# Side stages of the ten half-size-product steps put into other slots of a hand-ordered transformer kernel

## The reference, cut to what matters

```python
x = x + _L0_xattn_ref(_layernorm(x), ctx_4096, ctx_4096, mask_BxSxS2_ff1, wq, wk, wv, wo)
x = x + _L0_ffn_ref(_layernorm(x), qweight_gu, ..., scales_down, g_idx_down)
x = x + _L1_xattn_ref(_layernorm(x), ctx_4096, mask_1x1xSxS2_ff0, ...)
x = x + _L1_ffn_ref(_layernorm(x), Wq, Wr, aux_keys, aux_values, ...)

# _L0_ffn_ref: 4-bit weights, 512 -> 2 x 1376 -> 512
w_gu = scales[g] * (nibble(qweight_gu) - zeros[g])        # 512 x 2752
gate, up = split(x @ w_gu)
h = silu(gate) * up
w_d = scales[g] * (nibble(qweight_down) - zeros[g])       # 1376 x 512
out = h @ w_d
```

## Time and profile before

| what | us |
|---|---|
| median of 3 runs (2410.39 to 2413.1) | 2411.44 |
| the profiled execution, time | 2413.45 |
| the profiled execution, span of the instructions | 2411.7 |
| mean granted TensorE clock | 0.993 of full speed |
| busy: VectorE, ScalarE, GpSimd | 1695.2, 1287.7, 1315.3 |

### The profile page before, as it was taken

The page is one execution under the profiler, slowest core; times in us unless marked ns, Lnnn a source line. Parts: engine busy times, 40 slices in busy tenths (PEclk is TensorE's granted clock), DMA queues, the critical chain, the costliest instruction groups (busy, mean ns, idle before and its releaser), DMA issues.

```text
span 2411.7 us, 46184 instructions
## 1 busy us (share of the span) xinstructions
PE 2356.1 (98%) x18020; PEld 1333.2 (55%) x18028; DVE 1695.2 (70%) x3229; ACT 1287.7 (53%) x2511; POOL 1315.3 (55%) x1069
## 2 busy tenths in 40 slices
PE   8899999999999999999989999999999999999998
PEld 4555555555555555444666655555555555555554
DVE  8877776777777788656777576666666666765666
ACT  7666555556555555434444554555555555544453
POOL 4556666666666666237843354445555555445631
PEclk9999999999999999999999999999999999999999
DMA  6111121312121111011102111122121212221101
GB/s 212 45 45 36 45 54 27 123 27 54 31 55 30 44 40 29 27 44 36 42 14 78 48 32 27 45 54 62 36 62 36 62 36 62 53 43 27 27 14 70
DMA packets 217911, 116.59 MB, mean 48 GB/s; under 512 B 169408, under 2 KB 192608, under 8 KB 216672
## 3 DMA queue, kind: packets, MB, share of 16 engines
q1 hardware_dynamic: 217696, 113.64, 18.5%
HBM read 65.81 MB, written 8.39 MB: 31 GB/s over the span
## 4 chain that ended last, share of the span: by engine, by line
PE 60%; POOL 15%; DVE 13%; ACT 6%; issue 5%; DMA 0%; SPq 0%; POOLq 0%; DVEq 0%; ACTq 0%
PE PB L945 17%; PE PB L897 16%; PE PB L881 6%; POOL AR L2933 5%; PE PB L1057 4%; PE PB L1114 4%; POOL AR L2938 4%; PE PB L1068 3%; POOL PSP L2951 3%; DVE WB L2115 2%; PE PB L922 2%; PE PB L987 2%; DVE AR L2313 2%; ACT JUNK L1455 1%; PE PB L853 1%
## 5 line engine op out<-in xcount | busy, mean ns | idle before, releaser
L945 PE MATMUL PB<-WB,AR 128*128 128x512 f16 x3072 | 683.3, 380 | 1.5 <-DVE AR L2313 1.1
L897 PE MATMUL PB<-XTB,WB 128*128 128x512 f16 x3072 | 681.0, 380 | 2.3 <-DVE WB L2115 1.3
L945 PEld LDWEIGHTS PB<-WB,AR 128*128 128x128 f16 x3072 | 297.8, 98 | 355.2 <-issue 5.9
L897 PEld LDWEIGHTS PB<-XTB,WB 128*128 128x128 f16 x3072 | 298.0, 98 | 347.7 <-issue 8.5
L2944 POOL TENSOR_TENSOR AR<-AR,SML 128x512 f32<-128x512 f32 x128 | 144.6, 1151 | 317.9 <-DVE SML L2298 317.9
L2328 DVE SCALAR_TENSOR_TENSOR X<-PB,SML,X 128x512 f32<-128x512 f32 x256 | 189.5, 747 | 170.1 <-PE PB L945 164.0
L1617 ACT ACTIVATE AR<-PB 128x512 f16<-128x512 f32 x256 | 131.3, 596 | 223.8 <-PE PB L987 223.8
L2208 DVE TENSOR_TENSOR AR<-PB,AR 128x512 f16<-128x512 f32 x128 | 88.2, 690 | 164.3 <-ACT AR L1580 164.3
L2933 POOL TENSOR_TENSOR AR<-AR,CST 128x512 f32<-128x512 f32 x128 | 183.0, 1429 | 31.3 <-ACT AR L1527 31.3
L1533 ACT ACTIVATE AR<-AR 128x512 f16<-128x512 f32 x128 | 80.5, 630 | 197.1 <-POOL AR L2938 195.7
L2179 DVE TENSOR_TENSOR AR<-AR 128x512 f16<-128x512 f32 x128 | 132.4, 1035 | 71.8 <-ACT AR L1533 71.8
(11 more groups left out here) (312 smaller groups left out, 4081.1 us busy)
## 6 DMA issues: line engine op xcount, KB each, us to landing
STG<-in_wo SPq DMA_DIRECT2D x14, 1024.0 KB
STG<-in_wq SPq DMA_DIRECT2D x13, 1024.0 KB
STG<-in_qw_gu SPq DMA_DIRECT2D x40, 128.0 KB
STG<-in_ctxT SPq DMA_DIRECT2D x4, 1024.0 KB
X<-in_x SPq DMA_DIRECT2D x4, 1024.0 KB, 10.4
kept<-CTB SPq DMA_DIRECT2D x4, 1024.0 KB, 8.2
CTB<-kept SPq DMA_DIRECT2D x4, 1024.0 KB, 6.2
out_x<-X SPq DMA_DIRECT2D x16, 256.0 KB, 2.4
```

Of the source, the lines that this page charges most:

```text
L897: m = pe.do.matmul(b[:, :], wq[x][:, k, h * 128:(h + 1) * 128], XT[y][c][:, k, :], start=n == 0, stop=n == 11)
L945: m = pe.do.matmul(b[:, :], AT[x][:, h, t * 128:(t + 1) * 128], wo[y][:, h, :], start=n == 0, stop=n == 11)
```

## The change

Six tables of slots are changed, and nothing else. By engine queue:

- `unpack_d` of the second half of blocks 3 and 4 goes from slot (s,3,2) to (s,3,3), s = 2 and 3.
- Token sums of chunk 0: `fold_x` goes from (2,0,2) and (2,0,3) to (2,0,3) and (2,1,1), `fold_x_hi` from (2,1,1) to (2,1,3), `fold_x_lo` from (2,1,2) and (2,1,3) to (2,2,0) and (2,2,1).
- Token sums of chunk 1: `join_x` goes from (2,3,0) and (2,3,1) to (2,2,3) and (2,3,0), `fold_x` from (2,3,2) and (2,3,3) to (2,3,1) and (2,3,2), `fold_x_hi` from (3,0,1) to (2,3,3), `fold_x_lo` from (3,0,2) and (3,0,3) all to (3,0,0).
- The weights w(1,0,1) and w(1,0,2) (s = 2 and 3): `scale` goes from (s,3,2) to (s+1,0,0), `low` from (s,3,3) and (s+1,0,0) to (s+1,0,1) and (s+1,0,3).
- The weight w(1,1,1): `amax` goes from (4,3,1) to (4,3,0).

```diff
-                plan_f(*(((0, 3, 3), (1, 0, 1))[j] if s == 0 else (1, 2 + j, 3) if s == 1 else (s, 3, 2 * j)), "unpack_d", s + 1, j)
+                plan_f(*(((0, 3, 3), (1, 0, 1))[j] if s == 0 else (1, 2 + j, 3) if s == 1 else (s, 3, 3 * j)), "unpack_d", s + 1, j)
...
-            (0, ((2, 0, 0), (2, 0, 1), (2, 0, 2), (2, 0, 3), (2, 1, 1)), ((2, 1, 2), (2, 1, 2), (2, 1, 3), (2, 1, 3))),
-            (1, ((2, 3, 0), (2, 3, 1), (2, 3, 2), (2, 3, 3), (3, 0, 1)), ((3, 0, 2), (3, 0, 2), (3, 0, 3), (3, 0, 3))),
+            (0, ((2, 0, 0), (2, 0, 1), (2, 0, 3), (2, 1, 1), (2, 1, 3)), ((2, 2, 0), (2, 2, 0), (2, 2, 1), (2, 2, 1))),
+            (1, ((2, 2, 3), (2, 3, 0), (2, 3, 1), (2, 3, 2), (2, 3, 3)), ((3, 0, 0), (3, 0, 0), (3, 0, 0), (3, 0, 0))),
...
-        for s in (1, 2, 3):
-            plan_prep_f(w(1, 0, s - 1), (s, 2, 3), (s, 3, 1), (s, 3, 2), (s, 3, 3), (s + 1, 0, 0))
+        plan_prep_f(w(1, 0, 0), (1, 2, 3), (1, 3, 1), (1, 3, 2), (1, 3, 3), (2, 0, 0))
+        for s in (2, 3):
+            plan_prep_f(w(1, 0, s - 1), (s, 2, 3), (s, 3, 1), (s + 1, 0, 0), (s + 1, 0, 1), (s + 1, 0, 3))
...
-        plan_prep_f(w(1, 1, 1), (4, 3, 1), (4, 3, 2), (4, 3, 3), (5, 0, 1), (5, 0, 2))
+        plan_prep_f(w(1, 1, 1), (4, 3, 0), (4, 3, 2), (4, 3, 3), (5, 0, 1), (5, 0, 2))
```

## The result

The changed kernel takes 2416.43 us (median of 17 runs, 2413.07 to 2418.51), the kernel before 2412.27 us on the same chip (17 runs, 2408.39 to 2416.33). The ratio is 1.0014, 95% interval 1.0007 to 1.0020: slower by 3.4 us, 1.7 to 4.8 (the two medians themselves lie 4.2 us apart). The forecast was 6.0 us faster. The profiled execution has a time of 2415.40 us, a span of 2413.6 and a mean granted clock of 0.994.

A forecast was written before the change was run, and what follows sets the result against it. TensorE, busy 98% of the span, bounds the kernel. -5.3 us at the end of (3,1), -0.9 at (4,0) and +0.2 for thin margins give -6.0: 2411.44 to 2405.4 us; 8-in-10 range 2401.0 to 2411.0.

The forecast's parts named there:

- The step that failed: (4,3): Step (4,3): the 1.1 us wait for the squares' load stays; DVE's queue shifts 3.4 us, costing nothing, at worst 1 us.
- The rival that ended slower: ScalarE's queue, scale delaying the copy of P5 in (3,0) and (4,0): +2.4 us, 2413.8; chance 0.12, 0.08 past the bound.
- the tables in (3,0), 0.7 us: In (3,0) the tables wait for banks 4 and 5 from 1195.4 until 1196.1, after DVE's unpack_d.
- 0.6 for a hidden quarter: Duration used for a hidden quarter on DVE: 0.6 us, with 0.69 as the mean, less where GpSimd is idle.
- The rival with stalls that cost the clock: Stalls of (3,0) longer or followed by half clock, 1.7 us a stretch: gain 2.5 to 4 us, 2408.2; chance 0.18.
- My reason against it: Against half clock in (3,0): in both stalls TensorE works at full rate before and after.
- The other stalls of (3,0): In (3,0) P7 waits 1.5 us for the P6 sum, and 2.5 us are lost waiting for the first down tile.
- 1190.0, as forecast: In (2,3) DVE adds P7 only after POOL's add_p5 ends at 1188.0; the three sums end at 1190.0.
- (4,0): The 0.9 us wait goes; scale delays the copy of P5 by 4.9 us, nothing lost, margin 0.6, up to 0.6 lost.
- waiting for TensorE again in (3,2): Later wants of (3,1) have 0.6 to 1.6 us to spare, and in (3,2) DVE waits for TensorE again.
- the removal: In (3,1) P6 follows P1 at once, at 1211.1 and full clock; the 36 matmuls are done 5.3 us ahead.
- Chunk 0: The 0.6 us wait in (2,1) goes; 4.8 us more on DVE in (2,2) are hidden, with margins of about 1 us.

The follow-up runs named there:

- experiment 3: The changed kernel with the small matmul of the first preparation (l1) in PSUM bank 5 instead of 4; ratio to the kernel before 0.9990.
- experiment 1: The changed kernel with the sum of squares of w(1,1,1) back in slot (4,3,1); ratio to the kernel before 0.9994.
- kernel 2: The kernel before with one edit alone, the sum of squares of w(1,1,1) moved to slot (4,3,0); ratio to the kernel before 1.0014.
- kernel 6: Experiment 1's kernel with scale and low parts of w(1,0,1) and w(1,0,2) back in their old slots; ratio to the kernel before 0.9991.
- experiment 4: Experiment 1's kernel with unpack_d of block 3's second half behind the sums' high parts in ScalarE's queue; ratio to the kernel before 0.9989.
- experiment 7: Experiment 1's kernel with unpack_d of the second half of blocks 3 and 4 back in slot (s,3,2); ratio to the kernel before 0.9982.
- Experiment 5: The kernel before with only the token sums of chunk 1 in their new slots; ratio to the kernel before 0.9990.
- experiment 9: The kernel before with only the token sums of chunk 0 in their new slots; ratio to the kernel before 1.0009.

## Why the prediction was wrong

**The step that failed: (4,3).** It said that moving `amax` ahead "does not move the landing, so the 1.1 us stay", that DVE's queue shifts by 3.4 us, and the P3 sum is just in time: "Nothing, at worst 1 us". That the shift reaches the P3 sum with next to nothing was right, by experiment 3. What was left out is a reader inside the shifted queue: DVE's reduction of the first small matmul, and the bank that the two small matmuls share. I followed the shift to the one place where a product's bank comes free and took it for the only one. It cost 4.8 us by the ledger, 1.3 of them the load's later landing in this execution, and 4.4 and 4.5 us by experiments 1 and 2. The rival that ended slower had the right mechanism, ScalarE's queue in front of the copy of P5, in the wrong step, (3,0), and by `scale` and not by a load.

**Mis-sized: the tables in (3,0), 0.7 us.** It came to 1.89 us of wait and 1.5 us of half clock (4.26 for 2.76). The cause of the longer wait is the term "0.6 for a hidden quarter"; this is read off the rows, no run was made for it. DVE's timeline of the changed kernel in (2,3), with the joins and differences running on GpSimd beside it (second fence):

```profile
1188.85 1.40 DVE L2445 SCALAR_TENSOR_TENSOR AR<-AR,SML 128x256 f32<-128x256 f32 x1
...
1190.77 0.89 DVE L2445 SCALAR_TENSOR_TENSOR AR<-AR,SML,WB 128x256 f32<-128x256 f32 x1
1191.58 1.49 DVE L2445 SCALAR_TENSOR_TENSOR AR<-AR,SML,PSP 128x256 f32<-128x256 f32 x1
```
```profile
1185.50 1.26 POOL L3037 TENSOR_TENSOR WB<-WB,PSP 128x512 f32<-128x512 f32 x1
...
1187.35 5.43 POOL L3016 TENSOR_TENSOR WB<-WB 128x512 f32<-128x512 f32 x4
```

The three take 3.78 us, 2.0 more than 3 x 0.6; the mean of the earlier trace rows hid that such an operation takes 0.5 us beside an idle GpSimd (at 1210.16 and 1212.05 of this trace) and 0.9 to 1.5 beside a busy one here, and the change moved GpSimd's work right beside them. I had used this contention for the low parts and not for the quarters. `unpack_d` then ended 1.6 us later than forecast, and the wait grew by 1.2, as P1 of (3,0) itself was 0.5 us late.

The Trainium skill (SBUF — State Buffer, "Who interferes with whom") says that a DVE operation with two SBUF inputs is held up by a GpSimd operation that reads SBUF. By that rule the quarters should stretch too, and these rows agree; I named the rule only for the low parts.

**Mis-sized: the clock.** The rival with stalls that cost the clock had 0.18 and a price of 1.7 us; it happened, behind the 1.89 us wait, at 1.5 us. In the stalls that follow at 0.53 and 1.69 us the clock stayed at 1.00. My reason against it, full rate before and after, did not hold. That the clock falls behind a wait of this size is not certain either: in (4,3) of kernel 6 TensorE waited 1.88 us, also from full rate, and the 36 matmuls behind it ran at 1.00 and took 3.93 us.

```profile
1308.31 0.22 PE L1004 MATMUL PB<-IDB,SML 128*128 128x128 bf16 x1 [1.88 <-ACT JUNK L1456]
```

The Trainium skill (TensorE: Matmul & The Clock Gate, "HAM oscillation — how this bites in real kernels") warns of longer idle gaps only, and by it the forecast would have stood; the 0.50 behind a wait of 1.89 us differs from it, and the measurement decides.

**The other stalls of (3,0)** came where forecast and shorter: 0.53 us for 1.5, and 1.69 for 2.5, as the tables had already eaten their part. By experiments 4 and 6 the down tile's is ScalarE's queue, as the prediction had it. `add_p5` ends at 1186.76 (1185.50 + 1.26), and VectorE's P7 sum starts 0.09 us behind it, at 1186.85 (the profile names no releaser there); the P3 sum is done at 1188.87. With the 1.14 us by which this execution came in earlier that is 1190.0, as forecast.

**(4,0).** The 0.9 us went, and 1.1 us came (1269.61), where the margin was given as 0.6 us. It takes two edits together, since neither experiment 6 nor 7 has it: `unpack_d`'s high part, now in slot (3,3,3), lets ScalarE copy P1 only at 1260.31, 2.7 us after P1's end, and `scale` follows with its 4.9 us as forecast. The prediction doesn't say when it had that copy start, so what it charged for the high part can't be read off it; the quarter behind them took 1.19 us, not 0.6, which alone uses up the margin. A loss of 0.7 us in (3,3) was not in the prediction: the small matmul's bank 4 is held by `unpack_d` for 0.31 us, and the down product starts 0.8 us after P2's end, where it was 0.1 (1246.78 now, 1250.20 before). Experiments 1, 3, 4 and 7 have this wait and 6 has not, so it comes with the move of `scale` and its low parts. The prediction had VectorE waiting for TensorE again in (3,2); in the trace it waits there only for ScalarE (1.18 us) and GpSimd (1.13 us), and is still behind in (3,3).

**Right:** the removal. The 5.3 us wait and the half clock in (3,1) went; P6 followed P1 at once, at 1212.00, which is 1213.1 on the clock of the kernel before (+ 1.14), 2.0 us behind the 1211.1 forecast. Experiment 5 shows it to be the work of the one row of chunk 1. **Chunk 0** was expected to be free and to bring 0.6 us; in experiment 9 it brings these and costs 1.6, of which 0.9 by the start of (3,0) and 0.6 in it. Its price on VectorE was forecast right: in the changed kernel VectorE leaves (2,2) at 1177.42, 1178.6 on the clock of before, as the prediction has it. What it left out is again the reader of a small matmul's bank, in (2,3).

**Open:** how much of the 3.4 us by the runs, against 2.8 by the trace, lies outside these steps, since each kernel was profiled in one execution; and why the clock fell behind 1.89 us of idle time in (3,0) and not behind 1.88 us in (4,3) of kernel 6.

## What to carry to other kernels

An in-order queue that meets a load has everything behind it at the landing's mercy. When an instruction that waits for a DMA is moved ahead, list every reader behind it on that engine and on the engines that follow it, the small ones too, and for each ask which buffer or PSUM bank it frees and who takes that next. And cost an operation by its duration beside the neighbour it will have, not by its mean.

## What the runs showed of the hardware

The clock fell behind shorter waits than I had thought, and not behind every one of them. It went to 0.50 after 1.89 us in (3,0), and after 3.88 us (kernel 2) and 4.58 us in (4,3), each time with TensorE at full rate before. Kernels 1, 4 and 6, with 1.92, 1.92 and 1.94 us in the place of the first, repeat it, with down products of 4.24, 4.23 and 4.16 us. It stayed at 1.00 after 1.69 us in (3,0), and after 1.79 us (kernel 3) and 1.88 us (kernel 6) in (4,3). The fall doesn't come at one fixed point: behind the 1.89 us the down product ran at 1.00 for its first 1.0 us and then at 0.50 to its end, and P7 behind it ran at 1.00; behind the 4.58 us the clock was at 0.50 from the first matmul, for about 2.5 us.

The load of 1024 columns (`in_wv`) took between 3.15 and 4.42 us from its start to its landing in ten kernels that don't touch it (3.15 before, 4.42 in the changed kernel, 3.54 to 3.94 in eight others), so a wait that hangs on it varies by over 1 us.
